# Three routed layers: each token group's gate product moved between the turnings of the groups behind it

## The chip, the cores and the metric

The program runs on one core of a Trainium2 chip. The metric is the device time of one execution in microseconds (us); lower is better. The core's engines work side by side and meet only at semaphores: TensorE (PE in the profile, its weight loads PEld), VectorE (DVE), ScalarE (ACT), GpSimd (POOL) and the DMA queues (SP issues most of them).

## The reference

Four transformer blocks run over 2 x 1024 = 2048 tokens of width 256. Each block adds an attention and a feed-forward part to the residual stream, each on a layer norm of it. Three of the four feed-forward parts are routed over 8 experts (256 to 1024 to 256), with different rules of choice. Cut to what is touched by the change:

```python
# block 1: two best experts of a token
h = _layernorm(x, ln2_g, ln2_b).reshape(B * S, D)
logits = h @ gate_w + gate_b
topv, topi = jax.lax.top_k(logits, TOPK)
...
# block 2: every expert whose sigmoid is over 0.5
probs = jax.nn.sigmoid(x_flat @ Wg + bg)
mask = (probs > THRESHOLD).astype(x_flat.dtype)
...
# block 3: the best expert alone
route = jax.nn.sigmoid(x @ Wr + br)
max_ind = jnp.argmax(route, axis=1)
```

The product with `gate_w`, `Wg` or `Wr` (256 x 8) is "the gate" here.

## The kernel before

`routed_layer` is called three times, as m1 (two best), m2 (threshold) and m3 (best one). Its beginning is this, and only this part is touched:

- The 2048 tokens are 16 tiles of 128, in four groups g of four tiles (CH = 512 tokens). VectorE normalises tile after tile into `xn` (L2158; `x_norm` in the profile) and counts each in `tile_normed`. In m1 the statistics of two groups, in m2 none and in m3 all are ready at the start; the missing ones come from GpSimd (L1962, L1964).
- TensorE turns (transposes) the tiles of a group once its four tiles are normalised: 8 turnings of 128 x 128 in float32 for each group (L2035), four into PSUM bank 2g and four into bank 2g + 1 (k = 0 and 1, the two halves of the width 256).
- ScalarE (L2296 with a gain and shift in m1, L2298 without) copies six of the eight turned banks to `xnT`. VectorE copies the two named in `DVE_TURNS`, (group 2, k = 1) and (group 3, k = 1), after all of its normalising (L2164 in m1, L2166 in m2 and m3). `evac_act` and `evac_dve` count the copies.
- The gate of group g is two float32 products (k = 0, 1) of the 128 x 32 `wide_gate` (the 8 gate columns, padded to 32) with 512 tokens. It writes partitions 32g to 32g + 31 of bank 0, so each group uses its own 32 columns of the array (L2043). It waits for the copies of groups 0 to g, and all gates wait for `wide_gate`, which GpSimd fills (L1965, L1968) after its own statistics work.
- The last gate counts `g_mm`. VectorE then copies bank 0 out (L2169), TensorE turns it back (L2048), and a long chain of small VectorE operations picks the experts, counts the tokens of each and writes the list of token ids (L2250). GpSimd gathers the rows of the first expert tiles by these ids, and the loop over expert tiles begins (L2079, L2088, L2097).
- `core.keep_busy` (L76) issues products whose result nobody reads, at points of the queue where TensorE would wait.

TensorE's queue is in program order, as every engine's. An instruction that waits for a semaphore holds all that stands behind it.

Of the kernel before, what the change touches and what calls it, by code (L numbers as in the profile page):

```python
# [27 lines left out]
NCH = TOK // CH  # L28
# [1792 lines left out]
def routed_layer(core, name, kind, src, stream, func, params, route, experts, fetched, ready, last=False):  # L1821
# [11 lines left out]
    with ExitStack() as ctx:  # L1833
# [51 lines left out]
        eps_done, rstd_done, tile_normed, gate_wide = sem("eps"), sem("rstd"), sem("normed"), sem("gate_wide")  # L1885
# [142 lines left out]
        @block.tensor  # L2028
        def _(pe):
            core.keep_busy(pe, 7, 2)  # L2030
            for g in range(NCH):
                pe.wait_ge(tile_normed, 4 * g + 4)
                for k in range(KD):
                    for j in range(4):
                        mm = pe.transpose(ps[:, 2 * g + k, j * P:(j + 1) * P], xn[:, 4 * g + j, k * P:(k + 1) * P], core.ident[:])  # L2035
                    mm.then_inc(transposed, 1)
            pe.wait_ge(gate_wide, 2)
            for g in range(NCH):
                pe.wait_ge(evac_act, turns_before(g, False))
                if turns_before(g, True):  # L2040
                    pe.wait_ge(evac_dve, turns_before(g, True))
                for k in range(KD):
                    mm = pe.matmul(ps[32 * g:32 * (g + 1), GATE_BANK, :], wide_gate[:, k, :], xnT[:, k, g * CH:(g + 1) * CH],  # L2043
                                   start=(k == 0), stop=(k == KD - 1))
            mm.then_inc(g_mm, 1)
            pe.wait_ge(logits_sb, 1)
            for j in range(4):
                mm = pe.transpose(ps[:, TURNED_BANK, j * P:(j + 1) * P], turned[:, j * P:(j + 1) * P], core.ident[:])  # L2048
# [6 lines left out]
            for t in range(NT):  # L2055
                mm = pe.matmul(counts[:, (t + 1) * EXPERTS:], ones_b[:], chosen[:, t, :].unsqueeze(1).broadcast_to([P, NT - t, EXPERTS]),  # L2056
                               start=False, stop=(t == NT - 1))
# [3 lines left out]
            mm = pe.matmul(ps[0:1, WHERE_BANK, 0:S + 2], route.unit[0:EXPERTS - 1], reached, start=True, stop=True)  # L2061
            if local:
                mm = pe.matmul(ps[0:1, WHERE_BANK, COLUMN_AT:COLUMN_AT + S + 2], room_of[0:EXPERTS - 1], reached, start=True, stop=True)
# [3 lines left out]
            for g in range(G):  # L2067
                pe.wait_ge(lanes_done, g + 1)
                for t in range(NT):
                    at = ps[:, TABLE_BANK, g * W:(g + 1) * W] if local else ps[:, TABLE_BANK, 0:W]  # L2070
                    mm = pe.matmul(at, lane_hits[:, g % 2, :, t], tokens_at[:, g, :, t],  # L2071
                                   start=(t == 0 and (local or g == 0)), stop=(t == NT - 1 and (local or g == G - 1)))
# [1030 lines left out]
```

## Time and profile before

| | |
|---|---|
| median of 3 runs | 2136.29 us (2133.60 to 2141.03) |
| the profiled execution | 2135.88 us |
| its span | 2134.1 us (1.8 us lie around it) |
| TensorE busy | 1990.0 us, 93% |
| VectorE, ScalarE, GpSimd busy | 49%, 44%, 34% |
| beginnings of the routed layers | at 904.9, 1274.6 and 1951.7 us of the span |

Durations of single instructions are in ns or us as the rows name them. TensorE's products overlap: the record of one begins before the record ahead of it has ended, so a block of n products is read by its first start and its last end. A float32 product that isn't a transpose leaves two records. A 16-record block of the gate is 8 products, and one group's gate is 4 records.

### The profile page before, as it was taken

What the parts mean: (1) busy time and instruction counts of PE and PEld (TensorE: products, weight loads), DVE (VectorE), ACT (ScalarE), POOL (GpSimd) and SP (SyncE); (2) the same over time, 40 slices, a digit from 0 to 9 for tenths busy, and PEclk for the clock granted to TensorE, in tenths of its full rate; (3) what the DMA queues carried; (4) which work ended last, traced back from release to release, by engine and by line L of the source; (5) the groups of instructions that cost most, each with busy time, mean ns of one, the idle gap of its engine ahead of it and who ended that gap; (6) DMA issues with size and microseconds to landing.
All of it is one profiled execution on the core that took longest, in us unless ns stands there. A gap on an engine that the chain in (4) does not pass through costs nothing. (4 is left out here: it accounts for less than half of the span.)

```text
span 2134.1 us, 39734 instructions
## 1 busy us (share of the span) xinstructions
PE 1990.0 (93%) x12586; PEld 1457.5 (68%) x12590; DVE 1045.7 (49%) x2419; ACT 933.7 (44%) x1932; POOL 718.8 (34%) x814
## 2 busy tenths in 40 slices
PE   6899999989999999889999888999999999798998
PEld 5576656642323222469999767999999999566997
DVE  6885853668777776352322255222222222586221
ACT  2422652257777777423333332333333333264232
POOL 0123972420000000224333242434333443595442
PEclk9999999998999999999999988999999999899999
DMA  5003300052111112254221164422222221602711
GB/s 170 20 1 131 129 4 0 1 168 57 39 50 46 39 39 71 69 191 137 34 35 33 30 209 156 124 35 34 35 36 35 35 35 30 191 21 61 234 32 23
DMA packets 124860, 150.44 MB, mean 70 GB/s; under 512 B 27638, under 2 KB 105303, under 8 KB 124749
## 3 DMA queue, kind: packets, MB, share of 16 engines
q1 hardware_dynamic: 93981, 116.61, 16.7%
q0 software_dynamic: 24288, 31.81, 8.9%
q8 instruction: 64, 1.05, 0.2%
q10 hardware_dynamic: 6480, 0.59, 0.2%
q14 instruction: 47, 0.39, 0.1%
HBM read 113.33 MB, written 37.38 MB: 71 GB/s over the span
## 5 line engine op out<-in xcount | busy, mean ns | idle before, releaser
L2088 PE MATMUL banks<-m_rowsT,x_normT 128*128 128x128 f32 x4032 | 472.9, 276 | 4.4 <-DVE m_rowsT L2276 2.5
L2088 PEld LDWEIGHTS banks<-m_rowsT,x_normT 128*128 128x128 f32 x4032 | 463.5, 193 | 18.9 <-DVE m_rowsT L2276 1.7
L2097 PE MATMUL banks<-m_experts,m_hT 128*128 x2016 | 455.7, 379 | 0.0
L2097 PEld LDWEIGHTS banks<-m_experts,m_hT 128*128 128x128 f32 x2016 | 373.3, 190 | 45.8
L2327 ACT ACTIVATE m_hT<-banks,m_bias 128x128 f32<-128x128 f32 x848 | 242.4, 369 | 246.0 <-PE banks L2088 246.0
L2003 POOL DMA_INDIRECT scratch_acc<-m_y,m_row_ids x106 | 171.3, 1616 | 403.3 <-ACT m_y L2337 365.8
L2798 ACT ACTIVATE sh_pT<-banks 128x1024 f32<-128x1024 f32 x256 | 250.8, 1023 | 27.0 <-PE banks L2759 27.0
L2276 DVE COPY m_rowsT<-banks 128x256 f32<-128x256 f32 x88 | 37.4, 425 | 413.1 <-PE banks L2079 413.1
L2337 ACT ACTIVATE m_y<-banks,m_weight 128x256 f32<-128x256 f32 x126 | 59.8, 474 | 351.4 <-PE banks L2100 288.7
L2822 DVE TENSOR_REDUCE sh_mhalf<-banks 128x1 f32<-128x512 f32 x308 | 194.2, 683 | 36.4 <-PE banks L2708 36.4
L2260 DVE TENSOR_SCALAR x_normT<-m_experts 128x2048 f32 x129 | 168.0, 1303 | 74.7 <-issue 69.9
L2759 PE MATMUL banks<-sa_qs,sa_ks 99*128 99x512 bf16 x512 | 153.7, 385 | 9.7 <-ACT sh_pT L2798 7.5
L1990 POOL DMA_INDIRECT m_rows<-scratch_rows,m_row_ids x114 | 124.2, 1089 | 99.1 <-POOL m_row_ids L1987 97.0
L2699 POOL TENSOR_TENSOR x_norm<-x_norm,sp_bo 128x256 f32<-128x256 f32 x16 | 11.6, 726 | 392.3 <-DVE sh_m L2832 392.3
L2708 PE MATMUL banks<-sa_ks,sa_qs 96*128 96x512 bf16 x410 | 136.6, 389 | 0.0
L2749 PE MATMUL banks<-sh_pT,sa_vh 128*17 128x512 f32 x1024 | 132.0, 597 | 1.2 <-ACT sh_pT L2798 1.2
L76 PE MATMUL banks<-ident 128*128 128x256 f32 x336 | 91.1, 423 | 37.0 <-PEq L1833 23.7
L2759 PEld LDWEIGHTS banks<-sa_qs,sa_ks 99*128 99x128 bf16 x512 | 41.4, 98 | 116.8 <-ACT sh_pT L2798 51.0
L2272 DVE TENSOR_SCALAR m_rowsT<-banks,m1p_gain,m1p_shift 128x128 f32<-128x128 f32 x76 | 27.7, 405 | 177.0 <-PE banks L2079 177.0
L76 PEld LDWEIGHTS banks<-ident 128*128 128x128 f32 x336 | 69.2, 213 | 51.6 <-issue 40.2
L2708 PEld LDWEIGHTS banks<-sa_ks,sa_qs 96*128 96x128 bf16 x410 | 40.4, 99 | 77.7 <-DVE sh_mhalf L2822 35.6
L2827 DVE CUSTOM_DVE_ANT_0 sh_rise<-banks,sh_rise 128x512 f32<-128x512 f32 x102 | 68.7, 688 | 35.5 <-ACT sh_rise L2786 35.2
(411 smaller groups left out, 2768.8 us busy)
## 6 DMA issues: line engine op xcount, KB each, us to landing
m_experts<-L_W SPq DMA_DIRECT2D x32, 1024.0 KB, 11.0
m_experts<-L1f_W SPq DMA_DIRECT2D x16, 1024.0 KB, 9.1
a_bt<-bias SPq DMA_DIRECT2D x16, 616.0 KB, 3.7
scratch_parts<-sp_part SPq DMA_DIRECT2D x16, 384.0 KB, 2.6
sa_qs<-scratch_parts SPq DMA_DIRECT2D x96, 64.0 KB, 2.3
scratch_rows<-x_norm SPq DMA_DIRECT2D x12, 512.0 KB, 3.4
sa_ks<-scratch_parts SPq DMA_DIRECT2D x90, 64.0 KB, 2.2
scratch_acc<-x_resid SPq DMA_DIRECT2D x8, 512.0 KB, 2.9
```

The source lines that it names most:

```text
L76: pe.matmul(self.ps[:, bank, 0:2 * P], self.ident[:], self.ident[:].unsqueeze(1).broadcast_to([P, 2, P]), start=True, stop=True)
L1990: pool.indirect_dma_start(rows[:, w % RING, :], None, table, bass.IndirectOffsetOnAxis(ap=row_ids[:, w:w + 1], axis=0), bounds_check=TOK, ...
L2003: pool.indirect_dma_start(stream, bass.IndirectOffsetOnAxis(ap=row_ids[:, w:w + 1], axis=0), y[:, w % RING, :], None, bounds_check=TOK - 1 ...
L2088: mm = pe.matmul(ps[:, H_BANK[u] + f // 4, f % 4 * P:(f % 4 + 1) * P], w1_tile[:, u, k, f * P:(f + 1) * P], rowsT[:, u, k, :], start=(k == ...
L2097: mm = pe.matmul(ps[:, Y_BANK[u], 0:D], hT[:, u, f, :], experts.w2[:, bass.ds(slot_of(e), 1), f, :], start=(f == 0), stop=(f == FB - 1 and ...
L2260: ins = dve.tensor_scalar(w1_tile[:, u, :, :], experts.w1[:, bass.ds(slot_of(e), 1), :, :].rearrange("p e k f -> p (e k) f"), 0.0, None, A ...
L2327: ins = act.activation(hT[:, u, f, :], ps[:, H_BANK[u] + c, j * P:(j + 1) * P], func, bias=bias[:, u, f:f + 1])
L2708: pe.matmul(ps[:, bank["a", s, c], :], qs[u][0:SR, h, t * P:(t + 1) * P], keys, start=True, stop=True).then_inc(a_mm, 1)
L2749: mm = pe.matmul(ps[32 * g:32 * g + DK + 1, O_BANK, :], vh[:, b * KT + k, head, :], pT[:, (2 * k + h) % 4, half, :], start=(k == 0), stop= ...
L2759: mm = pe.matmul(ps[:, B_BANK + 2 * (n % 2) + half, :], ks[u][:, h, k * P:(k + 1) * P], qs[u][:, h, half * CH:(half + 1) * CH], start=True ...
L2798: act.activation(pT[:, n % 4, :, :], ps[:, B_BANK + 2 * (n % 2):B_BANK + 2 * (n % 2) + 2, :], ACT.Exp, scale=DK ** -0.5).then_inc(exp_done, 1)
L2822: dve.tensor_reduce(mhalf[:, s % 2, half, col:col + 1], ps[:, bank["a", s, c], :], AX, ALU.max).then_inc(a_max, 1)
```

## The change

The turnings of a group and the gate of a group become two local functions, and the order in which TensorE's queue holds them is written out: turnings 0 and 1, gate 0, turnings 2, gate 1, turnings 3, gates 2 and 3. Before, all turnings stood ahead of all gates. The waits, operands and counts are the same ones; the one wait for `gate_wide` now stands ahead of gate 0, and with it ahead of turnings 2 and 3. No other engine's code is changed.

```diff
-            for g in range(NCH):
+            def turn_tokens(g):
                 pe.wait_ge(tile_normed, 4 * g + 4)
                 for k in range(KD):
                     for j in range(4):
                         mm = pe.transpose(ps[:, 2 * g + k, j * P:(j + 1) * P], xn[:, 4 * g + j, k * P:(k + 1) * P], core.ident[:])
                     mm.then_inc(transposed, 1)
-            pe.wait_ge(gate_wide, 2)
-            for g in range(NCH):
+
+            def gate(g):
                 pe.wait_ge(evac_act, turns_before(g, False))
                 if turns_before(g, True):
                     pe.wait_ge(evac_dve, turns_before(g, True))
                 for k in range(KD):
                     mm = pe.matmul(ps[32 * g:32 * (g + 1), GATE_BANK, :], wide_gate[:, k, :], xnT[:, k, g * CH:(g + 1) * CH],
                                    start=(k == 0), stop=(k == KD - 1))
+                return mm
+
+            turn_tokens(0)
+            turn_tokens(1)
+            pe.wait_ge(gate_wide, 2)
+            gate(0)
+            turn_tokens(2)
+            gate(1)
+            turn_tokens(3)
+            gate(2)
+            mm = gate(3)
             mm.then_inc(g_mm, 1)
```

TensorE's instructions at the beginning of m1 (m2 and m3 read alike), before; `x_norm` is `xn`, `x_normT` is `xnT`, `m_rowsT` the copied-out logits:

```order
L76 MATMUL banks<-ident 128x256 x2
L2035 MATMUL banks<-ident,x_norm 128x128 x32
L2043 MATMUL banks<-x_normT,m_wide_gate 32x512 x8
L2048 MATMUL banks<-ident,m_rowsT 128x128 x4
L76 MATMUL banks<-ident 128x256 x6
```

The 32 turnings stand in one piece, then the four gates of 2 products each in one piece. The same place in the changed kernel, whose lines are numbered up to 12 higher:

```order
L76 MATMUL banks<-ident 128x256 x2
L2036 MATMUL banks<-ident,x_norm 128x128 x16
L2044 MATMUL banks<-x_normT,m_wide_gate 32x512 x2
L2036 MATMUL banks<-ident,x_norm 128x128 x8
L2044 MATMUL banks<-x_normT,m_wide_gate 32x512 x2
L2036 MATMUL banks<-ident,x_norm 128x128 x8
L2044 MATMUL banks<-x_normT,m_wide_gate 32x512 x4
L2060 MATMUL banks<-ident,m_rowsT 128x128 x4
L76 MATMUL banks<-ident 128x256 x6
```

Two products of the gate have moved ahead of the turnings of group 2, two more ahead of those of group 3, and four stay behind them. Nothing else moved on this engine, and nothing on the others.

## Rows read from the trace of the kernel before

**Rows 1.** The profile's first lines: span, busy time and instructions of each engine.

```profile
span 2134.1 us, 39734 instructions
PE 1990.0 (93%) x12586; PEld 1457.5 (68%) x12590; DVE 1045.7 (49%) x2419; ACT 933.7 (44%) x1932; POOL 718.8 (34%) x814
```

**Rows 2.** Chain that ended last, stage m3: start us, us, what (engine, tile, line).

```profile
1951.69 1.39 DVE x_norm L2158 x4
1953.12 5.38 PE banks L2035 x32
1958.50 2.77 PE banks L2043 x16
1961.29 0.70 DVE m_rowsT L2169
1962.04 0.67 PE banks L2048 x4
```

**Rows 3.** Timeline of TensorE, m1: start us, us, engine, line; idle before in brackets.

```profile
906.34 1.09 PE L2035 MATMUL banks<-ident,x_norm 128*128 128x128 f32 x8 [0.34 <-DVE x_norm L2158]
907.63 1.09 PE L2035 MATMUL banks<-ident,x_norm 128*128 128x128 f32 x8 [0.20 <-DVE x_norm L2158]
908.99 1.09 PE L2035 MATMUL banks<-ident,x_norm 128*128 128x128 f32 x8 [0.26 <-DVE x_norm L2158]
910.27 1.09 PE L2035 MATMUL banks<-ident,x_norm 128*128 128x128 f32 x8 [0.19 <-DVE x_norm L2158]
911.30 2.94 PE L2043 MATMUL banks<-x_normT,m_wide_gate 128*32 128x512 f32 x16
```

**Rows 4.** Timeline of TensorE inside that gate block, cut to three narrow windows.

```profile
911.30 0.64 PE L2043 MATMUL banks<-x_normT,m_wide_gate 128*32 128x512 f32 x3
911.30 1.07 PE L2043 MATMUL banks<-x_normT,m_wide_gate 128*32 128x512 f32 x6
912.79 1.02 PE L2043 MATMUL banks<-x_normT,m_wide_gate 128*32 128x512 f32 x2
```

**Rows 5.** Timelines of ScalarE (first row) and VectorE in m1: copies of turned banks.

```profile
907.10 1.45 ACT L2296 ACTIVATE x_normT<-banks,m1p_shift,m1p_gain 128x512 f32<-128x512 f32 x2 [2.02 <-PE banks L2035]
911.41 0.81 DVE L2164 TENSOR_SCALAR x_normT<-banks,m1p_gain,m1p_shift 128x512 f32<-128x512 f32 x1 [0.40 <-PE banks L2035]
914.28 0.69 DVE L2169 COPY m_rowsT<-banks 128x512 f32<-128x512 f32 x1 [2.06 <-PE banks L2043]
```

**Rows 6.** Timeline of TensorE, attention of block 1, 706 us: narrow products, then full-width turnings.

```profile
705.66 1.05 PE L2749 MATMUL banks<-sh_pT,sa_vh 128*17 128x512 f32 x8
706.64 0.66 PE L2721 MATMUL banks<-ident,sh_oT 128*128 128x128 f32 x4
```

**Rows 7.** Timelines of TensorE (x16: window cut after group 1) and GpSimd, m2.

```profile
1277.72 3.49 PE L2035 MATMUL banks<-ident,x_norm 128*128 128x128 f32 x16 [2.03 <-DVE x_norm L2158]
1282.26 1.09 PE L2035 MATMUL banks<-ident,x_norm 128*128 128x128 f32 x8 [0.17 <-DVE x_norm L2158]
1283.28 2.82 PE L2043 MATMUL banks<-x_normT,m_wide_gate 128*32 128x512 f32 x16
1280.74 0.20 POOL L1968 COPY m_wide_gate<-m2p_wg 128x16 f32<-128x16 f32 x1
```

**Rows 8.** Timeline of TensorE, m3, window cut after the turnings of group 1.

```profile
1953.12 3.53 PE L2035 MATMUL banks<-ident,x_norm 128*128 128x128 f32 x16 [0.34 <-DVE x_norm L2158]
```

**Rows 9.** Busy time by window: window, us, busy (count) of each engine, granted clock, DMA.

```profile
1277.48:1280.90 3.42, 3.18 (x15) 3.18 (x16) 3.19 (x10) 1.49 (x3) 3.19 (x8) 0.50 0.69 233
1953.32:1956.73 3.41, 3.41 (x18) 3.41 (x17) 3.41 (x12) 1.80 (x4) 1.43 (x6) 0.50 0.81 268
929.32:936.15 6.83, 5.47 (x36) 4.69 (x34) 2.05 (x4) 0.00 (x0) 3.31 (x5) 0.50 0.07 20
1301.38:1318.44 17.06, 14.59 (x111) 12.77 (x110) 8.51 (x13) 0.00 (x0) 5.81 (x9) 0.50 0.20 59
1973.80:1977.21 3.41, 3.19 (x8) 2.60 (x9) 1.23 (x1) 1.28 (x1) 2.91 (x4) 0.50 0.14 40
```

**Rows 10.** Timeline of TensorE, m2: the first two blocks of expert products.

```profile
1314.77 5.57 PE L2088 MATMUL banks<-m_rowsT,x_normT 128*128 128x128 f32 x32 [0.52 <-DVE m_rowsT L2276]
1321.35 3.83 PE L2088 MATMUL banks<-m_rowsT,x_normT 128*128 128x128 f32 x32 [0.78 <-DVE m_rowsT L2276]
```

## The prediction

> **What bounds the kernel now.** I read the first lines of the profile, then the chain of work that ended last, then the timelines of the three beginnings. The span is 2134.1 us and TensorE is busy for 93% of it [rows 1], but that share says nothing of a stretch as short as this one. The chain does. In m3 it goes from the first normalised tiles through all 32 turnings, all 16 records of the gates and the copy of the logits, without a gap [rows 2]. Behind it comes the serial choice of experts, for which every engine waits. So a microsecond later at the end of the last gate is a microsecond later for the rest of that layer, and nothing catches it up: the gather, the first expert tile and the loop all hang on the list of ids. All three layers have this form.
>
> Within the beginning two things matter. First, in m1 TensorE is not the pace-maker of the turnings. Groups start at 906.34, 907.63, 908.99 and 910.27, each with a wait of 0.19 to 0.34 us for VectorE's normalising ahead of it [rows 3]. Those gaps look like room for a gate. Second, the gate block is far shorter than its parts. Three records start together at 911.30 and are done after 0.64 us, and the first six records take 1.07 us [rows 4]: the gates of groups 0, 1 and 2 run **at the same time**, each in its own 32 columns of the array, and the next record of a group comes 0.43 us (1.07 - 0.64) after the one before. Of the last gate the final two records take 1.02 us together, alone in the array [rows 4]: again 0.43 us from start to start and 0.59 for the last. So a gate takes the same time alone as in company: 3 x 0.43 + 0.59 = **1.88 us** for its four records.
>
> What ends last is the gate of group 3. It can't begin before VectorE has copied bank 7 out, at 911.41 + 0.81 = 912.22 [rows 5]. The block ends at 911.30 + 2.94 = 914.24 [rows 3], which is 912.22 + 0.15 (semaphore to start) + 1.88, rounded. The gates of groups 0 to 2 lie completely beside it and beside that copy. They cost the path **nothing** in the kernel before.
>
> **The change, part by part.** No instruction is added or removed. Gates 0 and 1 (4 records each) are moved ahead of turnings that lie on the path.
>
> *What is won:* the gates behind the last turning fall from four to two. By the last paragraph gate 3 alone sets the end there, so the gain is 0.
>
> *What is paid:* turnings use all 128 columns, so they can't run beside a gate, and TensorE's queue is in order. The price of one insertion comes from two switches. From turnings to gate: the last block of turnings ends at 910.27 + 1.09 = 911.36 and the gate starts at 911.30 [rows 3], 0.06 to 0.07 ahead of the end of the last record. From narrow products back to full-width turnings the routed layers show nothing. The nearest rows are in the attention of block 1, where 17-column float32 products in four column groups are followed by turnings of the same form: 705.66 + 1.05 = 706.71 against a start at 706.64 [rows 6], 0.07 ahead of the end. One insertion thus moves the next turnings to (end of the turnings before) - 0.07 + 1.88 - 0.07 = end + **1.74 us**. A block of 8 turnings then takes 1.09 us [rows 3].
>
> m1: turnings 1 end at 907.63 + 1.09 = 908.72 [rows 3]. Gate 0 needs both copies of group 0, done at 907.10 + 1.45 = 908.55 [rows 5], plus the 0.15 seen above: 908.70, just behind the 908.65 that the queue would allow. Turnings 2 start at 908.70 + 1.81 = 910.51 and end at 911.60; gate 1 starts at 911.53; turnings 3 start at 913.34 and end at 914.43. Before they ended at 911.36. **+3.07 us.** The gaps of [rows 3] have taken only some 0.8 of the 3.9 us.
>
> m2: turnings 0 and 1 end at 1277.72 + 3.49 = 1281.21 [rows 7]. The wide gate is ready at 1280.74 + 0.20 = 1280.94, so the wait that now stands ahead of turnings 2 costs nothing by itself, by a margin of 0.1 to 0.2 us. Gate 0 starts at 1281.14, turnings 2 at 1282.95, gate 1 at 1283.97, turnings 3 at 1285.78, ending at 1286.87. Before: 1282.26 + 1.09 = 1283.35. **+3.52 us.** Turnings 2 followed turnings 1 without any gap here.
>
> m3: turnings 0 and 1 end at 1953.12 + 3.53 = 1956.65 [rows 8]. The granted clock is 0.50 (1.2 GHz) until 1956.73 [rows 9], which stretches the first 0.15 us of gate 0 and adds about 0.08. Turnings 2 then start at 1958.47, gate 1 at 1959.49, turnings 3 at 1961.30, ending at 1962.39. Before, all 32 ended at 1953.12 + 5.38 = 1958.50 [rows 2]. **+3.89 us.** Here TensorE never waited for VectorE, so there is no gap to use.
>
> Behind the last turning all is as before: VectorE's copy of bank 7, 0.15 us, gate 3, with gate 2 beside it. Gate 2 starts right behind the turnings and its four records end 1.81 us after them, about 1.1 us before gate 3's. ScalarE's and VectorE's other copies move with their turnings and aren't late for anything else. SP's stores of `xn` hang on the normalising and don't move.
>
> Sum: 3.07 + 3.52 + 3.89 = **10.5 us**. Against the profiled execution that is 2135.88 + 10.5 = 2146.4. Its time is 0.4 us under the median of the runs shown, so by the median I would write 2146.8; I take 2146.5, 0.5% above.
>
> Bounds of the sum: if a switch were free, the turnings would start when the gate's last record has streamed, 0.59 - 0.43 = 0.16 us ahead of its end and not 0.07, and the gate as early behind its turnings. That is 0.19 us less for a gate, 1.1 for six: 9.4. If each switch waited for the record ahead to end, it would be 0.07 more at each of four switches a layer: 0.8 more, 11.3.
>
> *A rule of the Trainium skill, weighed.* The row for the switch is [rows 6]: full-width turnings start 0.07 us before the narrow record ahead has ended. The Trainium skill, "TensorEngine Tiling (Array Packing)", section "Key Properties", says that changing the tiling mode drains TensorE. It speaks against this change, which adds four such switches to a layer. By the rule the sum is the 11.3 us of the upper bound, by the row it is 10.5; the row has a duration, so it is used.
>
> **The rivals.**
> *A. Hidden, no change (0.09).* The gates fit into TensorE's waits for VectorE, or the time is given back further on. For it: the gaps of 0.19 to 0.34 us in m1. Against it: a gate takes 1.88 us, and m2 has one gap, m3 none. If they fitted, the time would be 2136. What could really give time back is the clock behind the beginning: it is at 0.50 in 929.32 to 936.15, 1301.38 to 1318.44 and 1973.80 to 1977.21 [rows 9], and the first expert block of m2 took 5.57 us in such a stretch against 3.83 for the next [rows 10]. If the shifted beginnings lost one or two of these stretches, 1.7 us each for an expert block and about as much for the filler ahead, 3 to 6 us would come back: 2141 to 2143, around the edge of what can be told. I have no row that says why they should go and not lengthen.
> *B. Faster (0.03).* The kernel before pays for four gates in company: if gate 3 were slowed by its neighbours, taking gates 0 and 1 from its side would shorten the end. It decides if a record step in company is over 0.43 us. Gate 3's steps are the same 0.43 alone [rows 4]. Had the four been serial, 4 x 1.72 = 6.9 us, the change would take 3.4 us a layer off the end and pay 3.5: no gain in m2 and m3 and 0.4 in m1. Faster by over 0.3% (6.4 us, about what a measurement of this kernel can tell from no change) it could be only with help from the clock: 2129.
> *C. Slower by more (0.10).* The half clock reaches further: gate 0 or 1 of m2 or m3 at 0.50 costs 1.7 us more each, or one more such stretch behind a beginning: 2148 to 2151.
> *D. The forecast (0.78).* +9.4 to +11.3, and the runs' own spread of a few microseconds: 2143 to 2149.
>
> **How the numbers follow.** Slower by over 0.3% is D without its low edge, and C: 0.84. Within 0.3%: A with that edge, 0.13. Faster: 0.03. The range 2141 to 2151 leaves out A's fully hidden case and B, and holds C.
>
> **What would show each step.** In the changed profile, m1: turnings x16, a gate block x4 of 1.88 us starting near 908.70, turnings x8 at 910.51, gate x4, turnings x8 at 913.34, and a gate block x8 whose end is near 917.3 where it was 914.24. VectorE's wait for the last gate stays at 2.06 us [rows 5]. Turnings that start less than 1.7 us after a gate would refute the serial price; a last gate block that shrinks by more than the copy allows would refute "gate 3 alone sets the end". The prediction is wrong in sign only if the time lost here is handed back behind the list of ids.

## The result, and the profile after

Over ten runs of each, before and changed kernel stand at 2134.94 us (2132.82 to 2141.03) and 2146.05 us (2142.56 to 2153.92). The ratio is 1.0044, 95% interval 1.0031 to 1.0056: the change costs some 9 us (6.6 to 12.0), the forecast was 10.5. At an equal mean granted clock of 0.978 three runs of the changed kernel stand at 2144.0 to 2144.2 us and eight of before, of another series, at 2134.2 on average: 9.9 us. The profiled execution of the changed kernel took 2143.96 us, its span is 2142.2 us, 8.1 more than before.

TensorE's timeline of the changed kernel in m1, m2 and m3 (start us, us, line; answers to [rows 2, 3, 7, 8]; the turnings are now L2036, the gates L2044):

```profile
903.82 1.09 PE L2036 MATMUL banks<-ident,x_norm 128*128 128x128 f32 x8 [0.34 <-DVE x_norm L2170]
905.11 1.09 PE L2036 MATMUL banks<-ident,x_norm 128*128 128x128 f32 x8 [0.20 <-DVE x_norm L2170]
906.58 1.90 PE L2044 MATMUL banks<-x_normT,m_wide_gate 128*32 128x512 f32 x4 [0.37 <-POOL m_wide_gate L1968]
908.41 1.09 PE L2036 MATMUL banks<-ident,x_norm 128*128 128x128 f32 x8
909.43 1.90 PE L2044 MATMUL banks<-x_normT,m_wide_gate 128*32 128x512 f32 x4
911.27 1.09 PE L2036 MATMUL banks<-ident,x_norm 128*128 128x128 f32 x8
912.29 2.94 PE L2044 MATMUL banks<-x_normT,m_wide_gate 128*32 128x512 f32 x8
...
1278.70 3.57 PE L2036 MATMUL banks<-ident,x_norm 128*128 128x128 f32 x16 [2.03 <-DVE x_norm L2170]
1287.92 2.82 PE L2044 MATMUL banks<-x_normT,m_wide_gate 128*32 128x512 f32 x8
...
1956.97 3.62 PE L2036 MATMUL banks<-ident,x_norm 128*128 128x128 f32 x16
1960.52 2.26 PE L2044 MATMUL banks<-x_normT,m_wide_gate 128*32 128x512 f32 x4
1966.60 2.82 PE L2044 MATMUL banks<-x_normT,m_wide_gate 128*32 128x512 f32 x8
```

Two things are to be seen. A gate ahead of turnings takes 1.90 us, and the turnings start 1.83 us after its start. And the block of gates behind the last turnings, now two, takes the same 2.94 us in m1 as the four did [rows 3]: nothing was won there. VectorE's wait for it is unchanged too (compare [rows 5]):

```profile
915.27 0.69 DVE L2181 COPY m_rowsT<-banks 128x512 f32<-128x512 f32 x1 [2.06 <-PE banks L2044]
```

From the start of the first turnings to the end of the last gate, m1 took 914.24 - 906.34 = 7.90 us before and 915.23 - 903.82 = 11.41 now, **+3.51**; m2 8.38 and 12.04, **+3.66**; m3 8.13 and 12.45, **+4.32**. That is +11.5. It isn't caught up before the list of ids: from the end of the last gate to the end of the list (L2250 in the kernel before) it takes 17.61, 22.28 and 11.90 us in m1, m2 and m3 before and 17.58, 22.26 and 11.91 in the changed kernel, and in all ten traces below these agree within 0.1 us. Nor between the layers m1 and m2: from the last gate to m2's first turnings both kernels take 363.5 us.

The span grew by 8.1 only, because instructions that the change doesn't touch took other times: m1's first turnings start 2.52 us *earlier* than before, and between the last gate of m2 and m3's first turnings 0.8 us were gained. Of the first, the granted clock is the likely cause. Ahead of m1's first turnings 27.3 us stood at half clock (granted 0.50) before and 17.1 us in the changed kernel, and TensorE was busy for 832.69 and 829.89 us there with 4507 and 4508 records. One such stretch; the first row is of before, the second of the changed one (window, us, busy and count of the engines, granted clock, DMA share, GB/s):

```profile
502.66:509.48 6.82, 6.08 (x15) 2.15 (x16) 3.99 (x11) 4.03 (x5) 0.72 (x1) 0.50 0.00 0
```

```profile
502.66:509.48 6.82, 6.39 (x37) 1.83 (x35) 6.16 (x15) 5.62 (x8) 0.00 (x0) 1.00 0.01 2
```

Before, TensorE ran this stretch of block 1's attention at 0.50 (1.2 GHz): two products of `sa_qs` and `sa_ks` (99 x 512, bf16) take 1.06 us there and 0.60 in the changed kernel at full clock. The counts aren't of the same instructions: the changed kernel's 37 hold 16 records of narrow products. So single spans aren't compared below. I compare the beginnings inside the traces and, for the whole, the ratios of the runs.

### The profile page after: what moved, and what is told of

Read it like the earlier page. It is cut to its first block and busy times, and to the rows that moved or that the text cites. A ratio compares the mean times of both kernels' runs of the same rounds, so it can differ in the third digit from the quotient of the medians.

```text
span 2142.2 us, 39734 instructions
## 1 busy us (share of the span) xinstructions
PE 1998.7 (93%) x12586; PEld 1459.6 (68%) x12590; DVE 1045.4 (49%) x2419; ACT 932.5 (44%) x1932; POOL 716.1 (33%) x814
```

## The experiments

My theory, S: a narrow gate ahead of full-width turnings holds them up for its whole 1.8 us; behind the last turnings gate 3's chain sets the end and the other gates cost nothing. The rivals: W, the wait for the wide gate, now ahead of turnings 2, is what costs; P, each gate product costs its own time wherever it stands.

The table gives, for m1, m2 and m3, the us from first turnings to the end of the last gate, and the sum of the differences to before. Each comes from the first and last row of that stage's timeline. The last column is the ratio of the runs to those of before.

| kernel | m1 | m2 | m3 | sum of differences | ratio (95%) |
|---|---|---|---|---|---|
| before | 7.90 | 8.38 | 8.13 | | |
| changed | 11.41 | 12.04 | 12.45 | +11.5 | 1.0044 (1.0031 to 1.0056) |
| gate 0 alone ahead | 9.43 | 10.05 | 8.86 | +3.9 | 1.0020 (1.0006 to 1.0033) |
| gates 0 and 1 together ahead | 9.48 | 11.38 | 10.12 | +6.6 | 1.0013 (1.0001 to 1.0025) |
| wait alone | 7.90 | 8.37 | 8.10 | 0.0 | 1.0002 (0.9990 to 1.0013) |
| gate 0 twice, behind | 8.64 | 9.60 | 8.59 | +2.4 | 1.0030 (1.0016 to 1.0044) |
| gate 0 twice, ahead | 13.13 | 15.10 | 12.57 | +16.4 | 1.0074 (1.0057 to 1.0090) |
| half of gate 3 early | 7.37 | 8.11 | 7.10 | -1.8 | 0.9990 (0.9978 to 1.0001) |
| gates by tile, behind | 6.91 | 7.92 | 6.85 | -2.7 | 0.9991 (0.9978 to 1.0005) |
| gates by tile, between | 7.67 | 8.27 | 8.28 | -0.2 | 1.0003 (0.9991 to 1.0014) |

The granted clock moves m2 and m3 of single traces by a microsecond or so (below); m1 ran at full clock in all ten and is the cleanest column. m3 ran at full clock in four of them: gate 0 alone ahead, gate 0 twice ahead, half of gate 3 early, and gates by tile, behind. In before, 3.4 us of m3 stood at half clock, and from the first turnings to the first gate it took 5.31 us against 4.89 in half of gate 3 early. So in these rows some 0.4 us of m3's difference goes with before's own stretch at half clock.

**Gate 0 alone ahead.**

```diff
             turn_tokens(2)
-            gate(1)
             turn_tokens(3)
+            gate(1)
             gate(2)
```

> Order: turnings 0, 1, gate 0, turnings 2, 3, gates 1, 2, 3. Theory S (a gate in front of turnings holds them up for its full 1.8 us, the gates behind the last turning cost only gate 3): one insertion instead of two. m1 +1.1 to +1.5 us at the end of the last gate (gate 0 also waits for the wide gate, filled at 909.05 of the trace of before, and VectorE's pace absorbs some), m2 +1.6, m3 +1.9: +4.8 us in all, 2140 against 2135. Rival W (it is the wait for the wide gate, now ahead of turnings 2, that costs): the whole +11 us stays. Rival C (the time is the clock's, not the queue's): the gate blocks would not begin 1.8 us ahead of the next turnings, and the time would be anywhere between 2133 and 2146.

TensorE's timeline of this kernel in m1:

```profile
911.39 1.90 PE L2044 MATMUL banks<-x_normT,m_wide_gate 128*32 128x512 f32 x4 [0.37 <-POOL m_wide_gate L1968]
913.23 1.97 PE L2036 MATMUL banks<-ident,x_norm 128*128 128x128 f32 x16
```

Measured: m1 +1.53, m2 +1.67, m3 +0.73, together +3.9 where 4.8 was forecast, and 1.0020 (+4.3 us, 1.3 to 7.1). One insertion instead of two costs m1 less than half of the changed kernel's +3.51, with the wait for the wide gate in its place; W, by which the whole cost would stay, is out. So is C of the expectation: the turnings start 1.84 us after the gate (911.39 to 913.23). m3 lies 1.2 us below the forecast 1.9. At full clock its turnings wait for VectorE (0.20 us ahead of turnings 1) where before's didn't, so part of the gate falls into such waits, and some 0.4 us is in the half clock of before's own 8.13.

**Gates 0 and 1 together ahead.**

```diff
             turn_tokens(0)
             turn_tokens(1)
+            turn_tokens(2)
             pe.wait_ge(gate_wide, 2)
             gate(0)
-            turn_tokens(2)
             gate(1)
             turn_tokens(3)
```

> Order: turnings 0, 1, 2, gates 0 and 1, turnings 3, gates 2, 3. As many gate products lie ahead of the last turnings as in the changed kernel, but side by side in different columns. Theory S: both gates together take 1.9 us, as one does, so m1 +1.6, m2 +1.6, m3 +2.0 at the end of the last gate, +5.1 us in all, about 2140. Rival P (every gate product that stands ahead of turnings costs its own 0.43 us for each of its records, neighbours or not): the same +10.5 to +11 us as the changed kernel, 2146.

TensorE's timeline of this kernel in m1:

```profile
911.25 1.09 PE L2036 MATMUL banks<-ident,x_norm 128*128 128x128 f32 x8 [0.26 <-DVE x_norm L2170]
912.27 1.92 PE L2044 MATMUL banks<-x_normT,m_wide_gate 128*32 128x512 f32 x8
914.12 1.09 PE L2036 MATMUL banks<-ident,x_norm 128*128 128x128 f32 x8
```

Eight records take 1.92 us, as four do in the changed kernel (1.90), and m1 is +1.58, m3 +1.99, as S forecast. The same products that cost m1 3.51 us one after the other (0.4 of it the wait for the wide gate) cost 1.58 side by side: P is out. Eight records of one gate, in "gate 0 twice, ahead" below, take 3.62 us instead:

```profile
906.67 3.62 PE L2044 MATMUL banks<-x_normT,m_wide_gate 128*32 128x512 f32 x8 [0.37 <-POOL m_wide_gate L1968]
```

In m2 the clock stood at half for 6.1 us of the beginning and not 3.2 as in before, which goes with +3.00 there instead of 1.6. By the runs it is +2.8 us (0.2 to 5.3), with the forecast 5.1 at the upper end and the 6.6 of the one trace above it.

**The wait alone.**

```diff
             turn_tokens(0)
             turn_tokens(1)
             pe.wait_ge(gate_wide, 2)
-            gate(0)
             turn_tokens(2)
-            gate(1)
             turn_tokens(3)
+            gate(0)
+            gate(1)
             gate(2)
```

> Order of before (all turnings, then all gates), with only the wait for the wide gate moved ahead of turnings 2. Theory S: m1 turnings 2 start 0.1 us later and turnings 3 on time, m2 and m3 nothing: within 0.5 us of before, 2135. Rival W: the wait is what costs, +6 us or more of the 11.

Timeline of TensorE, m1:

```profile
909.79 1.09 PE L2036 MATMUL banks<-ident,x_norm 128*128 128x128 f32 x8 [0.20 <-DVE x_norm L2170]
911.26 2.27 PE L2036 MATMUL banks<-ident,x_norm 128*128 128x128 f32 x16 [0.38 <-POOL m_wide_gate L1968]
913.46 2.94 PE L2044 MATMUL banks<-x_normT,m_wide_gate 128*32 128x512 f32 x16
```

Turnings 2 do wait for GpSimd (0.38 us of idle time, where VectorE held them for 0.26 before), but turnings 3 catch up. The layers differ from before by 0.00, 0.01 and 0.03 us, the ratio is 1.0002. The wait by itself costs nothing, as long as no gate takes the slack behind it.

**Gate 0 twice, behind and ahead of turnings.** The second computation writes the same values to the same place. The first of the two kernels has the order of before, the second that of the changed kernel.

```diff
             pe.wait_ge(gate_wide, 2)
             gate(0)
+            gate(0)
```

> Order of before, with the two products of gate 0 computed twice behind the last turnings (the second time over the same place, the same values; 4 more records in a layer). Theory S (gates behind the last turnings run side by side, gate 3's chain sets the end at 2.87 us behind the last turning): gate 0's column group now streams 8 records, 3.43 + 0.1 us behind the last turning, so its end comes 0.6 to 0.7 us later in each layer: +2 us in all. Rival P (each product costs its own time wherever it stands): +1.7 us a layer, +5.1 us.

> Order of the changed kernel, with gate 0 computed twice where it stands ahead of turnings 2 (the same added work as in the run above). Theory S: nothing covers it, four more steps of 0.43: +1.71 us a layer over the changed kernel, +5.1 us in all, and from the start of the normalising to the list of ids m1 32.1, m2 37.5 and m3 27 to 28 us. A rival in which gates ahead of turnings are hidden in part would give less, 1 us a layer or under.

Ahead, m1 is +1.72 over the changed kernel (13.13 - 11.41), the forecast 1.71. m2 (+3.06, with 6.1 us of it at half clock where the changed kernel had 3.3) and m3 (+0.12, with none where it had 4.3) scatter around it; the three together are +4.9, the forecast 5.1. By the runs, 1.0074 (six runs) against 1.0044 is +6.4 us, and the two intervals leave about 2 to 11. From the start of the normalising to the list of ids it took 32.16, 38.82 and 25.93 us: the forecast met m1 (32.1) and missed m2 (37.5) and m3 (27 to 28), the two with the other clock. Behind, it costs +0.74 us in m1, and from the last turning to the last gate 3.62 us in m2 and 3.61 in m3 where it was 2.75. So the same work costs 1.7 us ahead and 0.7 to 0.9 behind. The size is the forecast one, but the reason was not the one that I gave. Timelines of TensorE, m1, three narrow windows:

```profile
917.60 1.90 PE L2044 MATMUL banks<-x_normT,m_wide_gate 128*32 128x512 f32 x4
918.91 1.08 PE L2044 MATMUL banks<-x_normT,m_wide_gate 128*32 128x512 f32 x5
920.20 1.08 PE L2044 MATMUL banks<-x_normT,m_wide_gate 128*32 128x512 f32 x8
```

I had expected gates 1 to 3 beside the first computation, with gate 0's eight records ending last. Instead its first four ran alone, from 917.60 to 919.50. Then the second computation and gates 1, 2 and 3 started together at 919.34 (five records in the second window: the fourth of the first computation, then four more), and the block ended with them. In the kernel before, gates overlapped with three waiting records of each earlier gate ahead of them in the queue; here, with more than three of one gate, they did not. Why the fifth record ends the hold is not shown. The runs say +6.4 us (3.4 to 9.4) where the three beginnings give 2.4. Some 2 us of that go with the granted clock: at a mean of 0.975 three runs of this kernel average 2143.5 us and five of before 2139.5, at 0.978 one stands at 2138.8 and nine of before average 2134.3, so at equal clock the difference is 4 to 4.5. The other 2 us, and why more of its runs had a lower clock, stay open.

**Half of gate 3 early.** The wait for VectorE's copies stands ahead of a gate's second product only.

```diff
                 pe.wait_ge(evac_act, turns_before(g, False))
-                if turns_before(g, True):
-                    pe.wait_ge(evac_dve, turns_before(g, True))
                 for k in range(KD):
+                    own = turns_before(g, True) if k == KD - 1 else turns_before(g - 1, True)
+                    if own:
+                        pe.wait_ge(evac_dve, own)
```

> Order of before, but the wait for VectorE's copies stands ahead of each gate's second product (k = 1) only, so that gate 3's first product may start when ScalarE has copied bank 6. If gate 3's chain behind VectorE's last copy sets the end: the start moves from 912.36 to 911.90 in m1 and by 0.54 us in m2 and m3: -0.5 us a layer, -1.5 us in all, visible in the trace, hardly in the times. If all four gates together set it: no change.

Timeline of TensorE, m1:

```profile
912.24 1.09 PE L2036 MATMUL banks<-ident,x_norm 128*128 128x128 f32 x8 [0.19 <-DVE x_norm L2171]
913.27 2.41 PE L2045 MATMUL banks<-x_normT,m_wide_gate 128*32 128x512 f32 x16
```

The block shrinks from 2.94 to 2.41 us with all four gates in it, and from 2.82 to 2.21 in m2 and m3. So gate 3's start behind VectorE's copy sets its length, and not the number of gates: with two in it (changed) or three (gate 0 alone ahead) it kept 2.94 and 2.95. The three blocks give -1.75 us, the forecast was -1.5; the whole is -1.8 in the trace, and the runs can't tell it from no change (0.9978 to 1.0001).

**Gates by tile, behind the turnings and between them.** Each group's gate becomes four products of 128 tokens for each k, one in each column group, and the logits are read back in the other order of group and tile. The second kernel has the changed kernel's order.

```diff
                 for k in range(KD):
-                    mm = pe.matmul(ps[32 * g:32 * (g + 1), GATE_BANK, :], wide_gate[:, k, :], xnT[:, k, g * CH:(g + 1) * CH],
-                                   start=(k == 0), stop=(k == KD - 1))
+                    for j in range(4):
+                        mm = pe.matmul(ps[32 * j:32 * (j + 1), GATE_BANK, g * P:(g + 1) * P], wide_gate[:, k, :],
+                                       xnT[:, k, (4 * g + j) * P:(4 * g + j + 1) * P], start=(k == 0), stop=(k == KD - 1))
...
-            logits = ps[:, TURNED_BANK, :].rearrange("p (j g c) -> p g j c", j=4, c=32)[:, :, :, 0:EXPERTS]
+            logits = ps[:, TURNED_BANK, :].rearrange("p (g j c) -> p g j c", j=4, c=32)[:, :, :, 0:EXPERTS]
```

> Order of before, but each group's gate is cut into its four token tiles, which run side by side in the four column groups (8 products of 128 tokens instead of 2 of 512; the same logits at other places of bank 0). Theory S: gate 3, alone behind VectorE's last copy, shrinks from 1.88 us to about 0.6 (4 steps of 0.11 and a last record of 0.27); gates 0 to 2 now take 1.3 to 1.5 us together and end about 0.3 us behind that copy. So the last gate ends 0.8 to 1.2 us earlier in each layer: -2.4 to -3.6 us, 2132. Rival (the end is set by all four gates' products together, not by gate 3's chain): 32 smaller products in place of 8 take as long or longer, no change or up to +1.5 us.

> Order of the changed kernel with the gates cut by token tile, four products side by side in all column groups. Theory S: an inserted gate now holds the columns for 4 x 0.11 = 0.44 us instead of 1.71, and with the switches the turnings behind come about 0.6 us later each; the last two gates end 0.1 us after gate 3 may start. m1 +0.9 - 1.25, m2 and m3 +1.25 - 1.25 against before: within 0.5 us of before a layer, in all -1 to +1 us of before and about 10 us under the changed kernel. Rival (the cost of the change is in the switches between narrow and full products, or in the semaphores, not in the streamed columns): it stays 5 us or more over before.

Timeline of TensorE, m1; first the kernel with all gates behind:

```profile
913.92 1.09 PE L2036 MATMUL banks<-ident,x_norm 128*128 128x128 f32 x8 [0.19 <-DVE x_norm L2171]
914.94 1.96 PE L2045 MATMUL banks<-x_normT,m_wide_gate 128*32 128x128 f32 x64
```

then the one with the gates between:

```profile
906.45 0.64 PE L2045 MATMUL banks<-x_normT,m_wide_gate 128*32 128x128 f32 x16 [0.38 <-POOL m_wide_gate L1968]
907.02 1.09 PE L2036 MATMUL banks<-ident,x_norm 128*128 128x128 f32 x8
908.04 0.64 PE L2045 MATMUL banks<-x_normT,m_wide_gate 128*32 128x128 f32 x16
908.62 1.09 PE L2036 MATMUL banks<-ident,x_norm 128*128 128x128 f32 x8
```

Behind, 64 small records take 1.96 us where 16 large ones took 2.94, and 1.96 and 1.95 in m2 and m3 where it was 2.82. The three blocks give -2.7 us, as do the three beginnings, and the forecast was -2.4 to -3.6; 0.9991 in the runs is again within what they can tell.

Between, one gate costs the turnings 0.57 us (906.45 to 907.02) and not 1.83. Against before, the shorter end makes up for two of them: -0.2 us, ratio 1.0003, as forecast, and the rival by which 5 us or more would stay is out. Against the same cut with all gates behind, the order of the changed kernel still costs 2.5 us in the three beginnings (-0.2 against -2.7), some of it by the clock of m3, where 3.4 us stood at half between and none behind; in m1, at full clock, it is 0.76. The insertions cost 11.5 us with whole gates. The switches and semaphores are the same in number, so together they can be no more than a part of the 0.57. The rest of the 1.83 us goes when a gate fills all four column groups: what costs is the columns left empty while it streams.

The fastest in the traces is the cut by tile with the order of before. It is faster than the changed kernel without overlap of the intervals. That it beats the kernel before rests on its three beginnings alone.

## Why the prediction was right

**The chain and the gain of nothing** held: the gate block behind the last turnings kept its 2.94 us in m1 with two gates less, and the half of gate 3 taken early showed what does shorten it. One row was misread on the way. The two records of 1.02 us at 912.79 [rows 4] end at 913.81, and the block ends at 914.24: they are gate 3's second and third, and the other gates' last records still run beside the second. The last two start at 913.22 and take 1.02 us too, so the steps of 0.43 us hold in company and alone. "Nothing catches it up" held as well, by the constant time from the last gate to the list of ids.

**The price of an insertion** held: 1.81 us from a gate's start to the next turnings was forecast, 1.83 measured. The switch measured in another part of the program [rows 6] carried over: the turnings start 0.07 us ahead of the gate's recorded end (906.58 + 1.90 = 908.48 against 908.41), and the 0.02 us are in the gate, 1.90 and not 1.88. At the switches neither bound came: two records of one gate overlap by 0.16 us (0.59 - 0.43), so a switch costs 0.09 us more than streaming on, and 0.07 less than waiting for the recorded end. The 11.5 us of the three beginnings lie above the upper bound of 11.3 for other reasons, which follow.

**m1** was forecast at +3.07 and measured at +3.51. The step that fell short is "gate 0 needs both copies of group 0": it needs the wide gate as well, and in m1 that came later. GpSimd filled it at 906.32 + 0.20 = 906.52 in the changed kernel's trace, and gate 0 started at 906.58, with 0.37 us of idle time ahead of it. By the trace of before it was to be seen: filled at 909.05 there, 2.7 us after the first turnings, as in the changed kernel. The prediction took GpSimd's time from m2 only. This term is the 0.40 us by which gate 0 started later than forecast, and two gates of 1.90 us give the rest of the 0.44. The experiment with the wait alone shows that this wait costs only together with the gate.

**m2** was forecast at +3.52, measured +3.66: its turnings 0 and 1 took 3.57 us and not 3.49, each gate 0.02 more. **m3**, forecast +3.89, was +4.32, because the clock stood at half for longer there: 1954.45 to 1961.28 in place of [rows 9]' 1953.32 to 1956.73. Gate 0 took 2.26 us and not 1.90. How far a half-clock stretch reaches into a beginning was not forecast beyond the stretch of the trace before. Window, us, busy time of the engines, granted clock of the changed kernel:

```profile
1954.45:1961.28 6.83, 6.15 (x21) 4.78 (x22) 5.60 (x18) 3.83 (x6) 2.67 (x7) 0.50 0.79 267
1305.92:1319.57 13.65, 11.20 (x96) 9.32 (x95) 7.22 (x11) 0.00 (x0) 3.87 (x6) 0.50 0.07 21
```

**Rival A** (time handed back by the clock) came true in a small way: m2's long stretch at half clock behind the beginning lasts 13.65 us and not 17.06 [rows 9]. It lies where the 0.8 us between m2 and m3 were gained; that it is their cause I have not shown. Nor is the shorter stretch shown to come from the insertion: with the order of before it lasted 17.1 us in the trace of the wait alone and 13.7 in half of gate 3 early. Over ten runs it does not cancel the loss: +11.1 us between the medians, +9 by the ratio.

**The number.** The median, 2146.05, lies 0.4 us from the forecast 2146.5, and that is luck: the interval is 5 us wide, the beginnings of the one trace sum to 11.5 us and not 10.5, and single runs of either kernel lie 8 us and more apart (2132.82 to 2141.03 and 2142.56 to 2153.92).

## What to carry to other kernels

An engine's idle gap takes up no more of an inserted piece of work than its own length: of m1's two gates of 1.83 us the gaps of 0.26 and 0.19 us took up only so much. And products that use a part of the array's columns (here 32 of 128, in separate groups) are nearly free beside their like, and cost their full length between full-width ones: move them in groups, or cut them so that each group fills all columns. Work that already runs beside the last step of a chain gains nothing by being done earlier.

## What the runs showed of the hardware that I had not expected

- The first records of three gates start within 0.03 us of each other (the three take 0.64 us [rows 4], the first record of a gate alone 0.62 in "gate 0 twice, behind"), although each gate's four records stand one behind the other in the queue. So TensorE starts a later gate's product, in other columns, ahead of an earlier gate's that waits for its own. That TensorE's queue is in program order, as is said of the kernel before, holds for what stands behind a wait for a semaphore, and not for the starts of such products. With eight records of one gate ahead (gate 0 twice, behind) the later gates waited until the fifth had started.
- The same instructions ahead of m1 took from 902.25 us (gates by tile, between) to 911.20 us (gate 0 twice, behind) until VectorE's first normalising, over the ten traces. In the windows of these two the same 4507 records kept TensorE busy 9.1 us longer in the second, at a lower granted clock: 37.5 us of it stood at half clock, and 17.1 us of the first (window, us, busy time and count of the engines, granted clock, DMA share, GB/s); a change of a few microseconds is therefore read inside its stage, not from a span.

```profile
0.00:902.25 902.25, 828.93 (x4507) 424.93 (x4508) 621.52 (x1430) 489.17 (x688) 213.72 (x277) 0.99 0.19 61
```

```profile
0.00:911.20 911.20, 838.01 (x4507) 428.47 (x4508) 622.27 (x1429) 489.43 (x688) 213.66 (x277) 0.98 0.19 60
```
